# Edge pass: the last group's sum stands ahead of this group's build and shares its signal; the round of pairs signals once

## The chip, the cores and the metric

One Trainium2 chip, one of its cores. The metric is the device time of one execution in microseconds. The times before are 1935.26, 1936.90 and 1938.03 us, median 1936.9.

## The reference, cut to what matters

Four layers of a graph network work on 3125 nodes of 128 features and 103125 edges that are sorted by destination. The kernel's edge pass computes layer 0's edge part, and beside it the matrix of edge counts and weights between nodes that layers 1 to 3 use.

```
h = maximum(layernorm(x), 0)                                   # 3125 x 128
msg_input = concatenate([h[src], h[dst], edge_attr])           # 103125 x 288
t = relu(msg_input @ W1.T + b1)
messages = t @ W2.T + b2
agg = segment_sum(messages, dst, num_segments=3125)
upd = relu(agg @ Wu.T + bu)
x = x + layernorm_with_gamma_beta(h + upd)
...                                                            # layers 1 to 3: segment_sum(h[src], dst) and
                                                               # segment_sum(w * h[src], dst), matmuls, norms
```

## The kernel before

Before the edge pass the node products P = h @ W1 (source part) and Q = h @ W1 (destination part) are made and stored as pairs of f16 halves. The edge pass (`edge_pass`) then runs over 202 groups (`MG`) of 512 edges, four blocks of 128, and at the same time over 196 rounds (`J`) of pairs, one round for 16 destination nodes. Behind the groups come 9 more steps (`LAST`) for the last node tiles. Every engine has its own stream with a loop `for s in range(MG + LAST)`, and the order in each stream is written out by hand; engines meet at semaphores only.

In step s:

- POOL gathers the source rows of a group with four indirect DMAs (line 989), five groups ahead (`SLOTS_P`); `gather(g)` waits until `pre` tells that the build of group g - 5 is done.
- TensorE: `build(s)` makes the messages before the relu in one of two PSUM banks: 8 matmuls of 128x128 (line 1309) for the attributes and the destination side, then 2 of 128x512 (line 1314) that add the gathered rows through the identity. It waits for `cut` of group s - 2, which frees the bank, and signals `pre`. `multiply(s)` makes the round's matrix with 8 matmuls of 128x150 (line 1327) in three units of 3, 3 and 2; each unit goes to one of four PSUM banks in turn and signals `multiplied`. From the second unit on it waits for `weights_out` of the round before. `sum_up(s - 1)` adds the messages of the group before into a band of 64 destinations with 8 matmuls of 128x64 (line 1339), one PSUM bank for all groups. It waits for `cut` of its group, and for `added` of the group before its own, and signals `summed`.
- ACT: `matrix_out(s - 1)` reads the three units out of PSUM (lines 1236, 1241, 1244), then `relu(s)` (line 1228) makes the high half of the messages. Then it stores the round's weights by DMA.
- DVE: `hots(s + 1)` (lines 1007, 1009), `whole_weights(s - 1)` (line 1034, three), `pair_hots(s + 1)` (lines 1022, 1024, 1027, 1028), `low_parts(s)` (line 1043, signals `cut`), `add(s - 1)` (line 1054, signals `added`), in every fourth step `ea_low` (line 1062). For each of 25 node tiles `update`, `residual`, `normalise` and `low_of_tile` follow 2, 4, 6 and 8 steps after the tile's last group; `update` begins at line 1102 and `residual` at line 1116.
- SP loads the sides, bands, attributes and tile rows; its loads of sides and bands wait for `pre`.

After the edge pass come the later layers, which no line of the change touches.

Of the kernel before, what the change touches and what calls it, by code (L numbers as in the profile page):

```python
# [29 lines left out]
MG = -(-E // GE)  # L30
# [21 lines left out]
UNITS = -(-PAIRS // UNIT)  # L52
# [34 lines left out]
def blocks_of(g):  # L87

    return min(MB, USED - g * MB)
# [680 lines left out]
def edge_pass(nc, new, d):  # L770

    NS, NPRE, NPG, NAB = 3, 2, SLOTS_P, BANDS_HELD
    with ExitStack() as ctx:
# [44 lines left out]
        aw_stored = [new(f"aw_stored{k}") for k in range(3)]  # L818
        hot_t, hot_ds = new("hot_t"), new("hot_ds")
        equalled, hot_keys = new("equalled"), new("hot_keys")  # L820
        pre, relued, cut, summed, added = new("pre"), new("relued"), new("cut"), new("summed"), new("added")
        multiplied, halves_out, weights_out, counted = (new("multiplied"), new("halves_out"), new("weights_out"),
                                                        new("counted"))
        dve_step, flagged, checked, cleared = new("edge_dve"), new("flagged"), new("checked"), new("edge_cleared")
# [8 lines left out]
        def in_twos(grid):  # L833
            return grid.rearrange("p a (e o) -> p a e o", o=2)

        def every_row(row, n):
            return row.rearrange("p (a e o) -> p a e o", a=1, o=2).broadcast_to([P, n, row.shape[1] // 2, 2])

        def every_column(column, width):
            return column.rearrange("p a (e o) -> p a e o", e=1).broadcast_to([P, column.shape[1], width // 2, 2])  # L840
# [29 lines left out]
        for name, row in (("lo", iota_lo), ("band", iota_band), ("key", iota_key)):  # L870
            width = row.shape[1] // 2
            held_rows[name] = (psum[:, 7, at:at + width], row[:, :].bitcast(F32))
            at += width
        row_lo, row_band, row_key = (held_rows[name][0].bitcast(F16) for name in ("lo", "band", "key"))

        def whole_at(t):
            past = EDGE + (t + 1) * P
            return 1 + max(g for g in range(MG) if base_of(g) + EDGE < past)
# [14 lines left out]
        with nc.Block() as block:  # L893
# [103 lines left out]
            def _(dve):  # L997
                def hots(g):
                    q, s = g // QUAD, (g // QUAD) % NS
                    n = blocks_of(g)  # L1000
                    if g >= 3:
                        dve.wait_ge(summed, g - 2)
                    dve.wait_ge(rel_in[q % 2], 16 * (q // 2 + 1))
                    if q >= NS:
                        dve.wait_ge(pre, QUAD * (q - NS + 1))
                    at = slice((g % QUAD) * GE, (g % QUAD) * GE + n * P)
                    nc.vector.tensor_scalar(side[2 * ED:P, s, at], rel_row[2 * ED:P, q % 2, at], band_no[2 * ED:P, 0:1],
                                            None, ALU.is_equal).then_inc(hot_t, 1)
                    nc.vector.tensor_tensor(in_twos(hot_d[:, g % 3, 0:n]), every_row(row_band, n),
                                            every_column(rel_of[:, g * MB:g * MB + n], BAND), ALU.is_equal  # L1010
                                            ).then_inc(hot_ds, 1)

                def pair_hots(r):
                    u = r % 2
                    if r >= 2:
                        dve.wait_ge(multiplied, UNITS * (r - 1))

                    def field(k, width):
                        return every_column(fields[:, k, r * PAIRS:(r + 1) * PAIRS], width)

                    equal, times_w1, times_w2 = (in_twos(hot_key[:, u, :, q, :]) for q in range(3))
                    nc.vector.tensor_tensor(equal, every_row(row_key, PAIRS), field(A_KEY, PKEY),
                                            ALU.is_equal).then_inc(equalled, 1)
                    nc.vector.tensor_tensor(in_twos(hot_lo[:, u]), every_row(row_lo, PAIRS), field(A_LO, P),  # L1024
                                            ALU.is_equal)
                    dve.wait_ge(equalled, r + 1)
                    nc.vector.tensor_tensor(times_w1, equal, field(A_W1, PKEY), ALU.mult)
                    nc.vector.tensor_tensor(times_w2, equal, field(A_W2, PKEY), ALU.mult).then_inc(hot_keys, 1)
# [9 lines left out]
                def low_parts(g):  # L1038
                    n = blocks_of(g) * P
                    if g >= 2:  # L1040
                        dve.wait_ge(summed, g - 1)
                    dve.wait_ge(relued, g + 1)
                    nc.vector.scalar_tensor_tensor(out=msg_lo[:, g % 2, 0:n], in0=pre_of(g), scalar=0.0,  # L1043
                                                   in1=msg_hi[:, g % 2, 0:n], op0=ALU.max,
                                                   op1=ALU.subtract).then_inc(cut, 1)

                def add(g):
                    dve.wait_ge(summed, g + 1)
                    if g:
                        dve.wait_ge(added, g)  # L1050
                    else:
                        dve.wait_ge(cleared, 1)
                    at = slice(base_of(g) + EDGE, base_of(g) + EDGE + BAND)
                    nc.vector.scalar_tensor_tensor(out=agg[:, at], in0=agg_of(g), scalar=1 / S_MSG, in1=agg[:, at],  # L1054
                                                   op0=ALU.mult, op1=ALU.add).then_inc(added, 1)
# [151 lines left out]
            def _(act):  # L1207
# [15 lines left out]
                def relu(g):  # L1223
                    n = blocks_of(g) * P
                    act.wait_ge(pre, g + 1)
                    if g >= 2:
                        act.wait_ge(summed, g - 1)
                    nc.scalar.activation(msg_hi[:, g % 2, 0:n], pre_of(g), ACT.Relu).then_inc(relued, 1)  # L1228

                def matrix_out(r):  # L1230
                    if r >= 3:
                        act.wait_ge(aw_stored[r % 3], 16 * (r // 3))
                    for j in range(UNITS):
                        unit = UNITS * r + j
                        act.wait_ge(multiplied, unit + 1)
                        nc.scalar.activation(columns_of_unit(flat_adj[:, :, r * W:(r + 1) * W], j), third_of(r, j, 0),  # L1236
                                             ACT.Copy, saturate=True)
                        if unit:
                            act.wait_ge(counted, unit)
                        n = len(pairs_of(j))  # L1240
                        nc.scalar.activation(over_of[:, 0:n * PKEY].rearrange("p (t a) -> p t a", t=NT),  # L1241
                                             third_of(r, j, 0), ACT.Relu, bias=minus_most[:, 0:1],
                                             accum_out=over[:, unit:unit + 1]).then_inc(counted, 1)
                        nc.scalar.activation(columns_of_unit(  # L1244
                            aw_out[:, r % 3, :].rearrange("p (t n) -> p t n", t=NT), j), third_of(r, j, 1), ACT.Copy,
                            scale=1 / UP).then_inc(halves_out, 1)
# [49 lines left out]
            def _(pe):  # L1296
# [21 lines left out]
                def multiply(r):  # L1318
                    u = r % 2
                    pe.wait_ge(hot_keys, r + 1)  # L1320
                    for j in range(UNITS):
                        unit = UNITS * r + j
                        if unit >= RING:
                            pe.wait_ge(weights_out, unit - RING + 1)
                        for i, p in enumerate(pairs_of(j)):
                            thirds = bank_of(r, j).rearrange("p (q x) -> p q x", q=3)
                            done = nc.tensor.matmul(thirds[:, :, i * PKEY:(i + 1) * PKEY], hot_lo[:, u, p, :],  # L1327
                                                    hot_key[:, u, p], start=True, stop=True)
                        done.then_inc(multiplied, 1)

                def sum_up(g):
                    n = blocks_of(g)
                    pe.wait_ge(cut, g + 1)
                    pe.wait_ge(hot_ds, g + 1)
                    if g:
                        pe.wait_ge(added, g)
                    for part, msg in enumerate((msg_hi, msg_lo)):
                        for k in range(n):
                            done = nc.tensor.matmul(agg_of(g), msg[:, g % 2, k * P:(k + 1) * P], hot_d[:, g % 3, k, :],  # L1339
                                                    start=(part == 0 and k == 0), stop=(part == 1 and k == n - 1))  # L1340
                    done.then_inc(summed, 1)

                def await_rows(s):
                    pe.wait_ge(hot_ds, min(s + 2, MG))
# [19 lines left out]
                    nc.tensor.matmul(psum[:, 7, 0:D], agg[:, at], w2u[:, :], start=True, stop=True).then_inc(u_psum, 1)  # L1364

                for s in range(MG + LAST):
                    if s < MG:
                        build(s)
                    if s < J:
                        multiply(s)  # L1370
                    if 1 <= s <= MG:
                        sum_up(s - 1)
                    if s == 2:
                        await_rows(s)
                        fold_weights()
# [1664 lines left out]
```

## Time and profile before

| | us |
|---|---|
| timed runs, median of 3 | 1936.9 (1935.26 to 1938.03) |
| profiled execution, its span | 2170.3 |
| of it: edge pass, groups 0 to 200 | 130 to 1358 |
| of it: later layers | 1378 to 2170 |

The profiled execution is one other execution, with the profiler writing a record of each instruction and each semaphore update. Durations of single instructions are read from it, and its 2170.3 us stand beside the 1936.9 of the timed runs. The two are not the same amount, so every sum is made against the profiled execution first. In the rows, the time in square brackets is the idle time of the engine before an instruction with what ended it; "remote" is a semaphore update for which no instruction ends near it, "issue" a wait for nothing that the profile shows. Ends of matmuls are modelled.

### The profile page before, as it was taken

What the parts mean: (1) busy time and instruction counts of PE and PEld (TensorE: products, weight loads), DVE (VectorE), ACT (ScalarE), POOL (GpSimd) and SP (SyncE); (2) the same over time, 40 slices, a digit from 0 to 9 for tenths busy, and PEclk for the clock granted to TensorE, in tenths of its full rate; (3) what the DMA queues carried; (4) which work ended last, traced back from release to release, by engine and by line L of the source; (5) the groups of instructions that cost most, each with busy time, mean ns of one, the idle gap of its engine ahead of it and who ended that gap; (6) DMA issues with size and microseconds to landing.
All of it is one profiled execution on the core that took longest, in us unless ns stands there. A gap on an engine that the chain in (4) does not pass through costs nothing. (4 is left out here: it accounts for less than half of the span.)

```text
span 2170.3 us, 30067 instructions
## 1 busy us (share of the span) xinstructions
PE 1378.5 (64%) x9130; PEld 904.1 (42%) x9130; DVE 1129.6 (52%) x3500; ACT 812.2 (37%) x3272; POOL 841.7 (39%) x877
## 2 busy tenths in 40 slices
PE   3235444445445454545545445799899999899997
PEld 2123233333333333333333333356656666455444
DVE  7756666667667666666666666431442224311101
ACT  2235455555545555454545544111343432100000
POOL 5636666666666666666666665000000000000001
PEclk8566766666666666666665666899999999899999
DMA  6444434434443433434434443103100001871770
GB/s 198 143 96 116 115 113 116 122 115 121 121 116 112 122 120 114 118 113 122 119 112 117 120 119 103 30 12 139 34 29 1 10 7 39 305 266 65 264 293 29
DMA packets 200853, 245.67 MB, mean 113 GB/s; under 512 B 36794, under 2 KB 174053, under 8 KB 200674
## 3 DMA queue, kind: packets, MB, share of 16 engines
q1 hardware_dynamic: 142978, 137.56, 20.1%
q0 software_dynamic: 29472, 65.73, 11.7%
q10 hardware_dynamic: 28224, 40.15, 5.2%
q8 instruction: 93, 1.52, 0.3%
q14 instruction: 86, 0.70, 0.1%
HBM read 174.00 MB, written 55.93 MB: 106 GB/s over the span
## 5 line engine op out<-in xcount | busy, mean ns | idle before, releaser
L989 POOL DMA_INDIRECT arena<-dram_PHL,src_of x786 | 765.2, 974 | 472.1 <-remote 205.4
L1327 PE MATMUL psum<-arena 128*128 128x150 f16 x1568 | 238.9, 294 | 604.3 <-DVE aw_out L1034 330.4
L1327 PEld LDWEIGHTS psum<-arena 128*128 128x128 f16 x1568 | 153.4, 125 | 762.2 <-issue 380.6
L1228 ACT ACTIVATE arena<-psum 128x512 f16<-128x512 f32 x202 | 121.9, 603 | 429.3 <-remote 294.5
L1236 ACT ACTIVATE arena<-psum 128x150 fp8e4<-128x150 f32 (+1 forms) x588 | 173.6, 295 | 181.4 <-remote 93.8
L1241 ACT ACTIVATE arena<-psum,arena 128x150 f16<-128x150 f32 (+1 forms) x588 | 228.6, 389 | 1.6 <-remote 1.6
L1309 PE MATMUL psum<-arena 128*128 128x128 f16 x1612 | 182.2, 281 | 39.0 <-DMA arena<-dram_QHL 36.3
L1054 DVE SCALAR_TENSOR_TENSOR agg_all<-psum,agg_all 128x64 f32<-128x64 f32 x202 | 43.8, 217 | 283.4 <-remote 281.4
L1314 PE MATMUL psum<-arena 128*128 128x512 f16 x404 | 184.5, 552 | 3.6 <-issue 3.6
L1244 ACT ACTIVATE aw_out<-psum 128x150 f32<-128x150 f32 (+1 forms) x588 | 179.6, 305 | 0.0
L1043 DVE SCALAR_TENSOR_TENSOR arena<-psum,arena 128x512 f16<-128x512 f32 x202 | 137.9, 683 | 76.2 <-issue 41.3
L2489 PE MATMUL psum<-arena,parts_b 128*128 128x512 fp8e4 (+5 forms) x875 | 172.1, 356 | 4.4 <-PEq L2911 3.8
L2452 POOL DMA_DIRECT2D parts_a<-dram_x x7 | 5.3, 752 | 419.6 <-DMA dram_x<-parts_a 396.3
L1309 PEld LDWEIGHTS psum<-arena 128*128 128x128 f16 x1612 | 144.4, 131 | 40.5 <-issue 38.8
L1034 DVE SCALAR_TENSOR_TENSOR aw_out<-psum,aw_out 128x150 f32<-128x150 f32 (+1 forms) x588 | 140.6, 287 | 11.7 <-issue 10.5
L2602 PE MATMUL psum<-arena,parts_a 128*128 128x512 f32 (+2 forms) x350 | 134.4, 544 | 2.4 <-ACT late_aggT L2727 2.4
L2602 PE MATMUL psum<-arena,parts_b 128*128 128x512 f32 (+2 forms) x350 | 133.0, 539 | 1.1 <-ACT late_aggT L2727 1.1
L1024 DVE TENSOR_TENSOR arena<-psum,fields 128x1024 f16<-128x1024 f16 x196 | 133.1, 679 | 0.0
L1241 ACT ACTIVATION_READ_ACCUMULATOR arena<-psum,arena 128x1 f32 x588 | 132.9, 226 | 0.0
L2489 PEld LDWEIGHTS psum<-arena,parts_b 128*128 128x128 f16 (+1 forms) x875 | 89.8, 104 | 77.6 <-issue 6.6
L1339 PE MATMUL psum<-arena 128*128 128x64 f16 x1612 | 111.0, 226 | 7.1 <-DVE agg_all L1054 7.1
L1339 PEld LDWEIGHTS psum<-arena 128*128 128x128 f16 x1612 | 102.1, 123 | 10.5 <-issue 6.9
(344 smaller groups left out, 2080.3 us busy)
## 6 DMA issues: line engine op xcount, KB each, us to landing
dram_aw<-aw_out ACTq DMA_DIRECT2D x196, 200.0 KB
arena<-dram_aw SPq DMA_DIRECT2D x6, 6400.0 KB
arena<-dram_aw SPq DMA_DIRECT2D x3, 4800.0 KB
arena<-in_ea_quads SPq DMA_DIRECT2D x51, 256.0 KB
arena<-dram_rel SPq DMA_DIRECT2D x51, 256.0 KB
arena<-arena SPq DMA_DIRECT2D x408, 32.0 KB
arena<-dram_PHL,src_of POOLq DMA_INDIRECT x806
arena<-dram_aw SPq DMA_DIRECT2D x2, 4000.0 KB
```

Source lines behind the costliest of these rows:

```text
L989: nc.gpsimd.indirect_dma_start(gathered_p[:, slot, k, :], None, d["PHL"], bass.IndirectOffsetOnAxis(ap=src_of[:, b:b + 1], axis=0)).then_i ...
L1034: nc.vector.scalar_tensor_tensor(out=columns_of_unit(whole, j), in0=third_of(r, j, 2), scalar=1 / UP, in1=columns_of_unit(whole, j), op0=A ...
L1043: nc.vector.scalar_tensor_tensor(out=msg_lo[:, g % 2, 0:n], in0=pre_of(g), scalar=0.0, in1=msg_hi[:, g % 2, 0:n], op0=ALU.max, op1=ALU.sub ...
L1236: nc.scalar.activation(columns_of_unit(flat_adj[:, :, r * W:(r + 1) * W], j), third_of(r, j, 0), ACT.Copy, saturate=True)
L1241: nc.scalar.activation(over_of[:, 0:n * PKEY].rearrange("p (t a) -> p t a", t=NT), third_of(r, j, 0), ACT.Relu, bias=minus_most[:, 0:1], a ...
L1244: nc.scalar.activation(columns_of_unit(aw_out[:, r % 3, :].rearrange("p (t n) -> p t n", t=NT), j), third_of(r, j, 1), ACT.Copy, scale=1 / ...
L1309: nc.tensor.matmul(out[:, k * P:(k + 1) * P], side[:, s, at:at + P], node_side[:, g % NAB, part * D:(part + 1) * D], start=(part == 0 and ...
L1314: done = nc.tensor.matmul(out, ident_h[:, :], gathered_p[:, g % NPG, 0:n, part * D:(part + 1) * D], start=False, stop=(part == 1))
L1327: done = nc.tensor.matmul(thirds[:, :, i * PKEY:(i + 1) * PKEY], hot_lo[:, u, p, :], hot_key[:, u, p], start=True, stop=True)
L1339: done = nc.tensor.matmul(agg_of(g), msg[:, g % 2, k * P:(k + 1) * P], hot_d[:, g % 3, k, :], start=(part == 0 and k == 0), stop=(part == ...
L2489: last = nc.tensor.matmul(psum[0:width, SUM_BANK[n % 2], 0:end - first], parts.flat[:, t * parts.block + at:t * parts.block + at + width], ...
L2602: last = nc.tensor.matmul(psum[:, 0, 0:m * W], g[k][:, t, :], slab[:, slot_of(n), 0:m, t * W:(t + 1) * W], start=(t == 0), stop=(t == NT - 1))
```

## The change

Four things change. (1) TensorE's loop calls `sum_up(s - 1)` ahead of `build(s)` and `multiply(s)`; before it stood behind both. (2) `sum_up` no longer signals `summed`. Since matmuls finish in order, the signal `pre` of the build that follows it tells of it too: `pre` of group g + 1 is the (g + 2)nd. `hots`, `low_parts` and `add` wait for that; only the last group, which no build follows, has a signal of its own (`last_sum`). (3) `relu` waits for `pre` alone. (4) `multiply` signals `multiplied` once for a round instead of once for a unit; `matrix_out` and `pair_hots` wait for the round.

```diff
@@ -872,6 +872,9 @@
+        def pre_with_sum(g):
+            return g + 2
@@ -999,7 +1002,7 @@
                     if g >= 3:
-                        dve.wait_ge(summed, g - 2)
+                        dve.wait_ge(pre, pre_with_sum(g - 3))
@@ -1013,7 +1016,7 @@
                     if r >= 2:
-                        dve.wait_ge(multiplied, UNITS * (r - 1))
+                        dve.wait_ge(multiplied, r - 1)
@@ -1038,14 +1041,17 @@
                     if g >= 2:
-                        dve.wait_ge(summed, g - 1)
+                        dve.wait_ge(pre, pre_with_sum(g - 2))
                     dve.wait_ge(relued, g + 1)
...
                 def add(g):
-                    dve.wait_ge(summed, g + 1)
+                    if g + 1 < MG:
+                        dve.wait_ge(pre, pre_with_sum(g))
+                    else:
+                        dve.wait_ge(last_sum, 1)
@@ -1223,16 +1229,14 @@
                     act.wait_ge(pre, g + 1)
-                    if g >= 2:
-                        act.wait_ge(summed, g - 1)
...
                 def matrix_out(r):
                     if r >= 3:
                         act.wait_ge(aw_stored[r % 3], 16 * (r // 3))
+                    act.wait_ge(multiplied, r + 1)
                     for j in range(UNITS):
                         unit = UNITS * r + j
-                        act.wait_ge(multiplied, unit + 1)
@@ -1326,7 +1330,7 @@
-                        done.then_inc(multiplied, 1)
+                    done.then_inc(multiplied, 1)
@@ -1338,7 +1342,8 @@
-                    done.then_inc(summed, 1)
+                    if g == MG - 1:
+                        done.then_inc(last_sum, 1)
@@ -1364,12 +1369,12 @@
                 for s in range(MG + LAST):
+                    if 1 <= s <= MG:
+                        sum_up(s - 1)
                     if s < MG:
                         build(s)
                     if s < J:
                         multiply(s)
-                    if 1 <= s <= MG:
-                        sum_up(s - 1)
```

## Rows read from the trace of the kernel before

**Rows 1.** Busy time by stage: stretch, length, each engine, granted clock, DMA
```profile
core 0: us, PE busy (x) PEld busy (x) DVE busy (x) ACT busy (x) POOL busy (x), PEclk, DMA share, GB/s
...
130.00:1358.00 1228.00, 590.86 (x5230) 426.36 (x5228) 813.53 (x2571) 618.88 (x2796) 765.24 (x786) 0.66 0.41 117
...
1378.00:2170.00 792.00, 748.28 (x3660) 447.81 (x3658) 211.54 (x659) 160.26 (x414) 12.84 (x16) 0.97 0.29 104
```

**Rows 2.** Waits of the edge pass: who waited for whom, total us, times, longest
```profile
ACT arena L1228 <- remote: 294.5, 118, 4.8
DVE agg_all L1054 <- remote: 281.4, 70, 7.3
...
POOL arena L989 <- remote: 205.4, 117, 3.1
```

**Rows 3.** Timeline of one step: start, us, engine, line, what [idle before, releaser]
```profile
659.69 0.39 PE L1339 MATMUL psum<-arena 128*128 128x64 f16 x8
...
663.15 0.30 ACT L1236 ACTIVATE arena<-psum 128x150 fp8e4<-128x150 f32 x1 [1.26 <-remote]
...
665.24 0.30 ACT L1236 ACTIVATE arena<-psum 128x150 fp8e4<-128x150 f32 x1 [1.25 <-PE psum L1327]
...
667.37 0.25 ACT L1236 ACTIVATE arena<-psum 128x100 fp8e4<-128x100 f32 x1 [1.28 <-issue]
...
668.87 0.23 DVE L1054 SCALAR_TENSOR_TENSOR agg_all<-psum,agg_all 128x64 f32<-128x64 f32 x1 [7.05 <-remote]
```

**Rows 4.** The gathers as a group: count, busy us, mean ns, idle before
```profile
L989 POOL DMA_INDIRECT arena<-dram_PHL,src_of x786 | 765.2, 974 | 472.1 <-remote 205.4 <-issue 196.1 <-PE psum L1314 70.6
```

**Rows 5.** Timeline of POOL: the first two gathers and the last
```profile
130.62 0.94 POOL L989 DMA_INDIRECT arena<-dram_PHL,src_of  x1 [21.92 <-PE psum L1314]
131.87 1.04 POOL L989 DMA_INDIRECT arena<-dram_PHL,src_of  x1 [0.30 <-issue]
...
1345.05 0.94 POOL L989 DMA_INDIRECT arena<-dram_PHL,src_of  x1 [0.31 <-issue]
```

**Rows 6.** Timeline of TensorE at the lower clock: sum, build's end, first unit
```profile
671.27 0.64 PE L1339 MATMUL psum<-arena 128*128 128x64 f16 x8
...
672.55 1.06 PE L1314 MATMUL psum<-arena 128*128 128x512 f16 x2
...
673.41 0.58 PE L1327 MATMUL psum<-arena 128*128 128x150 f16 x3
```

**Rows 7.** Timeline of ACT: a relu, then a round's first and last instruction
```profile
656.82 0.60 ACT L1228 ACTIVATE arena<-psum 128x512 f16<-128x512 f32 x1 [2.82 <-remote]
...
657.31 0.29 ACT L1236 ACTIVATE arena<-psum 128x150 fp8e4<-128x150 f32 x1
...
658.02 0.32 ACT L1236 ACTIVATE arena<-psum 128x150 fp8e4<-128x150 f32 x1
...
659.19 0.32 ACT L1244 ACTIVATE aw_out<-psum 128x100 f32<-128x100 f32 x1
```

**Rows 8.** Timeline of DVE over one step in which it hardly waits
```profile
657.52 0.69 DVE L1043 SCALAR_TENSOR_TENSOR arena<-psum,arena 128x512 f16<-128x512 f32 x1
658.13 0.21 DVE L1054 SCALAR_TENSOR_TENSOR agg_all<-psum,agg_all 128x64 f32<-128x64 f32 x1
...
659.72 0.35 DVE L1022 TENSOR_TENSOR arena<-psum,fields 128x400 f16<-128x400 f16 x1
...
661.14 0.68 DVE L1043 SCALAR_TENSOR_TENSOR arena<-psum,arena 128x512 f16<-128x512 f32 x1
```

**Rows 9.** Timeline of DVE: an update and a residual, each to the next group's work
```profile
673.10 0.33 DVE L1102 SCALAR_TENSOR_TENSOR tail_y<-b2u_rows,arena,bu_rows 128x128 f32<-128x128 f32 x1
...
674.78 0.35 DVE L1007 TENSOR_SCALAR arena<-arena 64x512 f16<-64x512 f16 x1
...
1345.71 0.15 DVE L1116 RECIPROCAL arena<-arena 128x1 f32<-128x1 f32 x1
...
1347.91 0.35 DVE L1007 TENSOR_SCALAR arena<-arena 64x512 f16<-64x512 f16 x1
```

More of the change, by code:

```diff
@@ L820, in edge_pass @@
         equalled, hot_keys = new("equalled"), new("hot_keys")
-        pre, relued, cut, summed, added = new("pre"), new("relued"), new("cut"), new("summed"), new("added")
+        pre, relued, cut, last_sum, added = new("pre"), new("relued"), new("cut"), new("last_sum"), new("added")
         multiplied, halves_out, weights_out, counted = (new("multiplied"), new("halves_out"), new("weights_out"),
```

## The prediction

> **What bounds the kernel now.** I read the stages first, then the waits of the edge pass, then the steps row by row. The stages [rows 1]: the edge pass is 1228 of 2170.3 us, 202 steps of 6.1 us, and no engine is full in it: DVE is busy for 814 us, POOL for 765, ACT for 619, TensorE for 591. The late layers take 792 us with TensorE busy for 748, and nothing of the change is in them. So the question is what a step waits for.
>
> The waits [rows 2] point at TensorE's signals: DVE stands 281.4 us before `add`, ACT 294.5 before `relu`, POOL 205.4 before a gather, each "remote", that is, a semaphore update with no instruction ending near it. In the rows of one step [rows 3] the eight matmuls of `sum_up` end at 660.08, and DVE, which waits for nothing but `summed`, begins `add` at 668.87. The multiplies of that round stand before the sum, so they too were done by 660; yet ACT, whose three units follow each other every 0.7 us where it is not held [rows 7], starts them at 663.15, 665.24 and 667.37. The matmuls were done and their signals came about 2 us apart. Five signals of TensorE leave a step (`pre`, three times `multiplied`, `summed`), and this is what the change goes at.
>
> **Does that queue of signals stand in the timed runs?** The profiled execution took 2170.3 us and the median of the timed runs is 1936.9: 233.4 us less. Where can they be missing? In the late layers TensorE is idle for only 792 - 748 = 44 us [rows 1]; those matmuls don't shrink. The 130 us ahead of the pass can give some 14 if they shrink as the whole did. So at least 175 of the 233 are missing from the edge pass, which then takes at most 1053 us, 5.2 per step. What would be left if no signal were late? The gathers: 786 of them [rows 4], the first starts at 130.62, the next 1.25 later, the last at 1345.05 [rows 5]. Back to back they take 1.25 us each when quiet, or the mean duration of 0.974 plus the 0.30 between two, 1.274: 982.5 to 1001 us, 5.0 to 5.1 per step. The last then ends at 1113 to 1132 instead of 1346.0, so 233 to 214 us earlier, and the execution takes 2170.3 - 233 = 1937 to 1956. The timed 1936.9 is the lower of these to half a microsecond. I take it that in the timed runs POOL issues gathers without a pause and the late signals are a product of the profiling. The Trainium skill fits that ("NOTIFIC — the notification-queue block", section "Overflow: three behaviours, one of which stalls the engine": the block's internal pipeline holds producers back rather than lose a record); no row here shows that block.
>
> **The change, part by part**, against 5.0 us per step of gathers.
>
> *One signal for a round's pairs.* TensorE gives 588 - 196 = 392 fewer increments, which costs it nothing. ACT starts `matrix_out` after the eighth matmul instead of the third: at the slow clock three take 0.58 us [rows 6], so five take 0.97. ACT's work for a round is 2.2 us (657.31 to 659.51) and its `relu` 0.6 [rows 7], 2.8 of a step of 5.0, so 0.97 is covered. DVE's `pair_hots` already needed all three units.
>
> *The sum ahead of the build, without a signal.* `sum_up` and `build` are the same instructions; only their order changes, no DMA moves with them, and 201 increments go. `hots`, `low_parts` and `add` wait for `pre` instead. `relu` has made DVE pass that value by the time of `low_parts`, so `add` waits for nothing more. The wait that is new in effect is TensorE's: `build(s)` stands behind `sum_up(s-1)`, which waits for `low_parts(s-1)` and for `add(s-2)`. Behind it are queued `multiply(s)`, and for `pre` wait `relu`, POOL's gather five groups on and SP's loads. The loops that this closes, with TensorE at the slow clock:
> - One step: `low_parts` to `add` 0.61 (657.52 to 658.13), `add` 0.21 [rows 8]; sum and build 671.27 to 673.61, 2.34 [rows 6]; `relu` 0.60, and 0.10 from its end to `low_parts` [rows 7, 8], taken for each of three hand-overs. 0.61 + 0.21 + 2.34 + 0.60 + 0.30 = 4.06.
> - Two steps, from a build's end: eight multiplies 1.55 (8/3 of 0.58), `matrix_out` 2.2, the last `whole_weights` about 0.2, `pair_hots` 1.42 (659.72 to 661.14), `low_parts` 0.61, `add` 0.21, sum and build 2.34, five hand-overs 0.5: 9.0, or 4.5 per step.
> - DVE alone: 3.62 from one `low_parts` to the next [rows 8]. An `update` adds 1.68 and a `residual` 2.20 [rows 9], each in 25 of 202 steps. Where these stand, the step is 0.82 + 2.8 + 1.7 or 2.2, about 5.3 and 5.8; with six others of 4.5, eight steps take 38.1, 4.76 per step.
>
> Before the change the first two loops aren't closed and DVE alone gives 3.62 + 0.124 x 3.88 = 4.1. So the change spends some 0.65 us per step, at the slow clock, of a slack of 0.9, and the gathers (1010 us for 202 steps, against 962) still come last. A gather waits for the build five groups back, so POOL doesn't feel one step of 5.8. Part sums: signals 0; later `matrix_out` 0; order 0. At the pass's end `sum_up(200)` leaves the place behind `build(201)`, at most 0.6 us, and it is hidden beside `relu`. Bounds: below, nothing but a late signal can be gained, 0 to 44 us (rival 1); above, 0 to 100 us (rival 2).
>
> **Rivals.** *1, faster:* some of the late signals are there without the profiler too. The pass could hold up to 44 us above the gathers if the late layers lost all their idle time in the timed runs. For: the rows show real waits. Against: the sum of the gathers leaves nothing. With half of it gone: 1936.9 - 22 = 1915. By the Trainium skill ("TensorE: Matmul & The Clock Gate", section "The cost: per-tile semaphore tail") increments of TensorE serialise at some 26 ns each; an estimate from that is 593 x 0.026 = 15 us if they were on the path, against 0 by my rows, where gathers cover them.
>
> *2, slower:* the new order becomes the bound: TensorE, held behind `sum_up(s-1)`, starts the build too late and POOL runs out of free slots. It decides from a mean step above 5.0, thus if a step costs 0.25 more than my 4.76. For: DVE's tile steps already stand above 5.0, and the clock was granted at 0.66, mostly the slow level [rows 1]. Against: all prices above are the slow clock's. At 5.15 per step it is 202 x 0.15 = 30 us: 1967. With only the 50 tile steps showing by 0.3 us: 1952.
>
> *3, it does nothing where it counts,* which is my forecast: the profiled execution gets shorter, since three of five signals are gone from each step, and the timed runs don't.
>
> **The numbers.** Forecast 1937 with 0.62 (within 0.2%, 1933 to 1941, about what a measurement of this kernel can tell from no change); rival 1 0.18; rival 2 0.20. The range goes to 1915 and 1960: it takes in half of rival 1, and of rival 2 what is below 0.11 us per step.
>
> **What would show it.** In the profile after: "remote" before `add` (281.4) near zero, as its wait is over before it; fewer of them before `relu` and POOL; the profiled span clearly shorter than 2170, between 1940 and 2100; POOL's 0.30 gaps in more of its rows. The forecast is wrong if the timed runs follow the profiled span downward (rival 1), or if the rows show TensorE idle before `sum_up` for `low_parts` or `add` while POOL waits for `pre` (rival 2).

## The result and the profile after

The changed kernel takes 1941.05 us (median of 20 runs, 1935.62 to 1944.54), the kernel before 1937.62 (20 runs, 1933.02 to 1941.11). The ratio is 1.0016, 95% interval [1.0009, 1.0023]: within the 0.2% that was forecast, and on the slow side of no change.

One fact has to stand ahead of every row, because the prediction missed it: the time of this kernel goes with the chip that it runs on. The kernel before took 1937.6, 1935.8, 1936.6 and 1939.4 us in four sets of runs, and 2157.4 (27 runs, 2152.8 to 2161.1) and 2172.7 (7 runs) on two other chips, where each of its runs was as long. By its length the profiled execution of before, 2170.3 us, belongs to the second kind of chip; which chip it ran on isn't on record. Its timed runs of 1936.9 and the profile after belong to the first. I call them the quick and the late kind. No chip was used at two separate times, so "chip" could also stand for something else that was the same through one set of runs.

The stages of the changed kernel's profile (stretch, length, busy time of TensorE, weight loads, DVE, ACT, POOL, granted clock, DMA):

```profile
core 0: us, PE busy (x) PEld busy (x) DVE busy (x) ACT busy (x) POOL busy (x), PEclk, DMA share, GB/s
130.00:1128.00 998.00, 611.73 (x5233) 430.54 (x5233) 819.48 (x2570) 619.62 (x2796) 753.05 (x786) 0.64 0.50 144
1149.00:1941.00 792.00, 747.88 (x3658) 447.64 (x3656) 211.58 (x659) 160.35 (x414) 12.84 (x16) 0.97 0.30 104
```

Beside [rows 1] the edge pass is 998 us instead of 1228, and the late layers are 792 as before (TensorE busy for 748 us in both). The gathers as a group (count, busy, mean ns, idle before), and the waits of the pass (who waited for whom, total us, times, longest), of the changed kernel:

```profile
L992 POOL DMA_INDIRECT arena<-dram_PHL,src_of x786 | 753.0, 958 | 265.9 <-issue 237.8
```

```profile
ACT arena L1232 <- PE psum L1318: 321.1, 173, 40.1
...
POOL arena L992 <- issue: 237.8, 780, 0.3
PE psum L1343 <- DVE agg_all L1060: 205.9, 185, 2.5
...
POOL arena L992 <- PE psum L1318: 28.2, 6, 24.0
```

Three things are to be seen. POOL's idle time is 780 gaps of 0.3 us, the issue itself: it gathers without a pause, where [rows 2] had it wait 205.4 us for signals. `relu` waits for the build and no longer for anything "remote". And the wait that the change creates is there: TensorE stands 205.9 us, in 185 of 201 steps, before `sum_up` for DVE's `add`, which follows `low_parts` directly. It costs POOL a pause in one place only (experiment 5).

The trace of the kernel before on a chip of the quick kind (experiment 5) is the right partner of this one. Its edge pass, in the window of the same length, and its waits, then `relu` over the whole pass (count, duration in ns, first and last start in us) in this trace and in the one that the prediction was read from:

```profile
130.00:1128.00 998.00, 571.98 (x5247) 428.78 (x5244) 821.54 (x2592) 608.21 (x2798) 750.81 (x786) 0.70 0.50 144
```

```profile
PE psum L1314 <- DMA arena<-dram_PHL,src_of: 309.1, 145, 4.6
...
POOL arena L989 <- issue: 237.2, 778, 0.3
...
DVE agg_all L1054 <- PE psum L1339: 0.6, 1, 0.6
```

```profile
L1228 ACT ACTIVATE arena<-psum x202: 383/597/761, 130.5 to 1123.7; 128x512 f16<-128x512 f32 x101
...
L1228 ACT ACTIVATE arena<-psum x202: 383/597/672, 130.4 to 1358.1; 128x512 f16<-128x512 f32 x101
```

The same kernel's pass is 993 us long on the one kind and 1228 on the other. From the last `relu` to the end it is 807 and 812 us, and the instructions themselves are as fast: the median `relu` is 597 ns in both, the median gather 944 ns.

So the kernel before, too, was already a row of gathers without a pause, TensorE waiting 309.1 us for their rows. On this kind of chip there was no late signal for the change to remove. In the changed kernel part of that idle time has only moved, from the wait for gathered rows to the wait for `add`.

### The profile page after: what moved, and what is told of

Same layout as the page of the kernel before. It is cut to its first block and busy times, and to the rows that moved or that the text cites. A ratio compares the mean times of both kernels' runs of the same rounds, so it can differ in the third digit from the quotient of the medians.

```text
span 1940.9 us, 29867 instructions
## 1 busy us (share of the span) xinstructions
PE 1399.7 (72%) x9130; PEld 908.6 (47%) x9130; DVE 1135.5 (59%) x3500; ACT 813.2 (42%) x3272; POOL 830.5 (43%) x877
## 5 line engine op out<-in xcount | busy, mean ns | idle before, releaser
L992 POOL DMA_INDIRECT arena<-dram_PHL,src_of x786 | 753.0, 958 | 265.9 <-issue 237.8
L1343 PE MATMUL psum<-arena 128*128 128x64 f16 x1612 | 104.4, 221 | 216.5 <-DVE agg_all L1060 206.7
L1331 PE MATMUL psum<-arena 128*128 128x150 f16 x1568 | 218.2, 307 | 43.2 <-DVE aw_out L1037 43.2
L1037 DVE SCALAR_TENSOR_TENSOR aw_out<-psum,aw_out 128x150 f32<-128x150 f32 (+1 forms) x588 | 150.5, 290 | 34.2 <-ACT aw_out L1248 28.2
L2732 ACT COPY late_aggT<-psum 128x512 f32<-128x512 f32 (+2 forms) x14 | 7.5, 533 | 255.0 <-PE psum L2607 255.0
```

The source lines that it names most:

```text
L992: nc.gpsimd.indirect_dma_start(gathered_p[:, slot, k, :], None, d["PHL"], bass.IndirectOffsetOnAxis(ap=src_of[:, b:b + 1], axis=0)).then_i ...
L1037: nc.vector.scalar_tensor_tensor(out=columns_of_unit(whole, j), in0=third_of(r, j, 2), scalar=1 / UP, in1=columns_of_unit(whole, j), op0=A ...
```

## The experiments

All ratios are to the kernel before on the same chip. Experiments 1 to 3 ran on the chip of 2157.4 us.

**1. The order alone**, all five signals kept. Late kind of chip.

```diff
+                    if 1 <= s <= MG:
+                        sum_up(s - 1)
                     if s < MG:
                         build(s)
                     if s < J:
                         multiply(s)
-                    if 1 <= s <= MG:
-                        sum_up(s - 1)
```

> The kernel before with one edit: TensorE calls sum_up(s-1) ahead of build(s); all five signals of a step stay. Theory A (the gathers bound the timed runs; the 3.4 us that the change adds are one pause of POOL before the gathers of group 9, 2.6 us in the profile after, because build(4) now stands behind the sum that waits for low_parts(3)): ratio 1.0015, about 1940.5 us timed, and a pause of 2 to 3 us of the same kind. Theory B (the added time comes with the changed signals): ratio 1.000. Of the profiled execution: if the late signals go by their number, its span stays above 2100 us, as five signals leave each step; if they go by the order, it falls to about 1941.

Measured: 2160.7 us against 2157.4, ratio 1.0015 [1.0006, 1.0024]. The number is that of theory A, but the ground had moved under it: this chip is late in every run, and on it POOL pauses in most groups, so the ratio can't be put down to the one pause of theory A. The span of 2156 us, against 2157.4 for the kernel before here, says that the order alone doesn't take the lateness away; of the profiler it says nothing. The order alone, with its gathers, was not run on a quick chip.

**2. The pairs' signal alone**, three signals a step. Same chip.

```diff
-                        dve.wait_ge(multiplied, UNITS * (r - 1))
+                        dve.wait_ge(multiplied, r - 1)
...
+                    act.wait_ge(multiplied, r + 1)
                     for j in range(UNITS):
                         unit = UNITS * r + j
-                        act.wait_ge(multiplied, unit + 1)
...
-                        done.then_inc(multiplied, 1)
+                    done.then_inc(multiplied, 1)
```

> The kernel before with one edit: multiply signals multiplied once for a round; the order and the signal of the sum stay, so three signals a step in place of five. Theory A: timed ratio 1.000 (0.999 to 1.001), as 0.97 us later in matrix_out is covered. Theory B: 1.001 to 1.002. Of the profiled execution: if the late signals go by their number, the span lies between 1937 and 2100 us, nearer to 1937; if they go by the order, it stays near 2170.

Measured: 2156.8 us, ratio 0.9997 [0.9987, 1.0007]. The later start of `matrix_out` is covered, and two signals fewer change nothing in the time. Waits of 200 to 1300 us, of the kernel before (the trace of 2170.3 us) and then of this one:

```profile
ACT arena L1228 <- remote: 270.7, 107, 4.8
...
DVE agg_all L1054 <- remote: 246.5, 62, 7.0
POOL arena L989 <- remote: 184.6, 106, 3.1
```

```profile
DVE agg_all L1054 <- remote: 251.8, 55, 6.7
ACT arena L1228 <- remote: 224.7, 101, 5.4
...
POOL arena L989 <- remote: 173.5, 103, 2.6
```

`add` waits as long as before, `relu` 46 us and POOL 11 us less. A queue of signals that went by their number would have given back far more: two of five are gone, and the time is the same.

**3. One load earlier**, in the changed kernel and in the kernel before. Late kind of chip.

```diff
+                        if q == 0:
+                            load_edges(2)
                         if q + 1 < QUADS:
                             load_sides(q + 1)
                             load_bands(q + 1)
                         if q + 2 < QUADS:
-                            load_edges(q + 2)
+                            if q:
+                                load_edges(q + 2)
```

> The changed kernel with SP's load of the attributes of quad 2 moved ahead of the loads of sides and bands of quad 1, in step 0 alone. In the profile after, ACT waits 4.5 us for these attributes and DVE 4.3 us for ACT, just ahead of the pause of POOL. Theory A: the pause of 2.6 us before group 9 goes, and the ratio to the kernel before is 1.000 (0.999 to 1.0005). If the cost is spread over the steps or stands at the end of the pass instead: it stays at 1.0016.

> The kernel before with the same move of the one load. Theory A: build(4) doesn't wait for low_parts(3) in the old order, so there is little or no pause to gain: ratio 1.000 (0.9993 to 1.0003). If the early load helps whatever the order: as much as it gives the changed kernel, some 0.9985.

Measured: the changed kernel with it 2166.5 us, 1.0045 [1.0031, 1.0058]; the kernel before with it 2158.3, 1.0002 [0.9993, 1.0011]. The first is a miss. On a chip where POOL pauses in most groups the one pause can't be seen, so the test was void there and was made again for the changed kernel (experiment 7); the kernel before with the early load has no run on a quick chip. It shows one thing more: with only two signals a step the changed kernel, with this load moved, is no quicker on the late kind of chip, at 2166.5 us it is slower than the kernel before. Why it was 0.3% slower than the order alone there is open.

**4. Three gathers a group instead of four**, in both kernels. The rows of every fourth block are left out and old ones used. A third chip, also of the late kind (the kernel before 2172.7 us).

```diff
+        def gathers_of(g):
+            return blocks_of(g) if g < NPG else min(blocks_of(g), 3)
...
-                    for k in range(blocks_of(g)):
+                    for k in range(gathers_of(g)):
...
-16 * sum(blocks_of(k) for k in range(g % NPG, g + 1, NPG))
+16 * sum(gathers_of(k) for k in range(g % NPG, g + 1, NPG))
```

> The kernel before, with three gathers in place of four for each group from the fifth on: the rows of every fourth block are left out (old rows of the slot are used in their place). POOL's floor falls from 5.0 to 3.8 us per step, so the other loops show. If the gathers bound the timed runs: the time falls until DVE's own 4.1 to 4.4 us per step is the bound, by 202 x 0.6 to 0.9 = 120 to 180 us, to 1757 to 1817. If they don't: it stays near 1937.

> The changed kernel with the same gathers left out. By the loops of the prediction (4.76 us per step with the sum ahead of the build, at the slow clock) the time falls by only 202 x 0.25 = 50 us, to about 1890, so 70 to 130 us slower than the kernel before with the same cut. If the loop with the sum ahead costs less than worked out there (the clock at its higher level, or hand-overs shorter): within 40 us of the kernel before with the same cut.

Measured: 1935.4 us, 0.891 [0.889, 0.893], and 1932.9 us, 0.889 [0.887, 0.891]. Both expected times are missed; what came true is the other branch of the second text, that the two kernels are within 40 us of each other. That the time with three gathers is the quick kind's time with four is chance: it is made of other steps. The stretch 200 to 1000 us, with four gathers (experiment 2's kernel, on the chip of 2157.4 us) and with three (the kernel before, on this chip):

```profile
200.00:1000.00 800.00, 375.88 (x3438) 271.07 (x3438) 541.83 (x1713) 406.53 (x1853) 508.54 (x524) 0.69 0.42 119
```

```profile
200.00:1000.00 800.00, 448.82 (x4191) 322.28 (x4190) 653.32 (x2089) 498.25 (x2273) 463.01 (x479) 0.71 0.46 132
```

524 gathers are 131 groups, 6.1 us each; 479 are 160 groups, 5.0 us each. The difference of 1.1 us is about one gather (1.25). On this kind of chip a step is the gathers' issue plus about 1.2 us: 4 x 1.25 + 1.1, 3 x 1.25 + 1.25 (the trace of 2170.3 us has 517 gathers in this stretch, 6.2 us a step). The rows of the kernel before show what the rest is. A step of its trace, on POOL, TensorE, ACT:

```profile
308.47 0.63 PE L1339 MATMUL psum<-arena 128*128 128x64 f16 x8
...
309.06 0.94 POOL L989 DMA_INDIRECT arena<-dram_PHL,src_of  x1 [0.31 <-issue]
...
309.68 0.59 PE L1314 MATMUL psum<-arena 128*128 128x512 f16 x2
...
311.35 0.60 ACT L1228 ACTIVATE arena<-psum 128x512 f16<-128x512 f32 x1 [3.89 <-PE psum L1314]
...
311.59 0.95 POOL L989 DMA_INDIRECT arena<-dram_PHL,src_of  x1 [1.59 <-PE psum L1314]
311.84 0.29 ACT L1236 ACTIVATE arena<-psum 128x150 fp8e4<-128x150 f32 x1
```

The build ends at 310.27, its signal reaches ACT at 311.35, 1.35 us after POOL's last gather ended, and the next gather follows at 311.59. In [rows 3] the queue is let go in the same way: POOL's last gather ended at 667.04, and at 668.87 to 669.04 came the sum, the build and a multiply together. I read this as theory C: beside gathers in flight TensorE's signals come late, they come through once POOL has to pause, and POOL pauses because it waits for one of them. It fits these rows and isn't shown, since no late chip ran without gathers.

**5. Both kernels again, unedited**, on a chip of the quick kind.

> The changed kernel, nothing edited, beside the kernel before on whatever chip this is. So far the kernel before took 1937 us on one chip and 2157 and 2173 on two others, all its runs alike, and there the order alone gave 1.0015, the pairs' signal alone 0.9997. Theory C (on some chips TensorE's signals don't get through while a gather is in flight, and POOL, once it waits for a build, lets them through; both kernels then run at four gathers and one flush per step): on such a chip the changed kernel takes 2155 to 2163 us, ratio 0.999 to 1.003, and its steps are 6.1 us; on the other kind 1941, ratio 1.0016. Against it (fewer signals help where signals are late): well under 2150 on a chip where the kernel before takes 2157 or more.

> The kernel before, nothing edited, for its own trace on this chip. On a chip of the 1937 kind: POOL's gaps of 0.30 in nearly all rows, relu within 0.1 us of the build's end, a pause of POOL before the gathers of group 9 shorter than the 2.6 us of the changed kernel by 2 to 3 us if that pause is the added time. On a chip of the other kind: the trace that the prediction was read from, 6.1 us per step, signals 2 us late.

Measured: the changed kernel 1940.8 us, 1.0026 [1.0017, 1.0035]; the kernel before as a kernel of its own 1937.7, 1.0009 [0.9998, 1.0021], which is how far the same kernel can stand from itself. POOL's waits for the build in the changed kernel (this is its second trace) and in the kernel before:

```profile
POOL arena L992 <- PE psum L1318: 28.5, 7, 23.2
```

```profile
POOL arena L989 <- PE psum L1314: 26.2, 8, 24.1
```

The longest is the start of the pass in both. What is left is 5.3 us in 6 waits and 2.1 us in 7, and 0.3 of each wait is the issue. In the changed kernel one row holds nearly all of it. Changed kernel, 144 to 155 us:

```profile
144.14 0.63 ACT L1219 ACTIVATE arena<-arena 128x512 f16<-128x512 f32 x1 [4.76 <-DMA arena<-in_ea_quads]
...
150.94 0.69 DVE L1046 SCALAR_TENSOR_TENSOR arena<-psum,arena 128x512 f16<-128x512 f32 x1
...
151.90 0.58 PE L1343 MATMUL psum<-arena 128*128 128x64 f16 x8 [1.82 <-DVE agg_all L1060]
...
152.30 1.04 PE L1313 MATMUL psum<-arena 128*128 128x128 f16 x8
...
153.13 1.06 PE L1318 MATMUL psum<-arena 128*128 128x512 f16 x2
...
154.46 0.94 POOL L992 DMA_INDIRECT arena<-dram_PHL,src_of  x1 [3.73 <-PE psum L1318]
```

Kernel before, the same groups:

```profile
142.24 0.63 ACT L1213 ACTIVATE arena<-arena 128x512 f16<-128x512 f32 x1 [5.97 <-DMA arena<-in_ea_quads]
...
149.03 0.69 DVE L1043 SCALAR_TENSOR_TENSOR arena<-psum,arena 128x512 f16<-128x512 f32 x1
...
149.24 1.06 PE L1314 MATMUL psum<-arena 128*128 128x512 f16 x2
...
149.95 0.94 POOL L989 DMA_INDIRECT arena<-dram_PHL,src_of  x1 [0.30 <-issue]
...
151.20 0.94 POOL L989 DMA_INDIRECT arena<-dram_PHL,src_of  x1 [0.30 <-issue]
```

In the kernel before the build of group 4 runs beside `low_parts(3)` and ends at 150.30, as POOL is in the last gather of group 8 (149.95 to 150.89); group 9 follows at 151.20 without a pause. In the changed kernel `sum_up(3)` has to come first, it waits for `low_parts(3)` and `add(2)`, and the build ends at 154.19. POOL, with its five slots used up, stands for 3.73 us before group 9, 3.43 more than its usual gap. It is the only such row of the pass; in the first trace it was 2.90, thus 2.6 more.

The new order is only half of why the build is 3.9 us later. From ACT's start on the attributes (144.14 and 142.24) to the end of build(4) it takes 10.05 us in the changed kernel and 8.06 before: these 2.0 us are the order's, nearly all of them the 1.82 us that `sum_up(3)` waits. The other 1.9 us are there already when the attributes arrive. SP sends for them behind four loads of bands, and these four took 3.35 to 3.80 us in all five traces with the new order on quick chips, and 2.5 us in the two with the old. Why they take longer is open.

The gathers themselves sum to 753.0 and 754.9 us in the changed kernel's two traces and to 750.8 here. With a single trace of the kernel before this can't be told from scatter.

**6. No gathers at all from the fifth group on**, rows of the first groups used again; the same two kernels, and then the order alone.

```diff
-            return blocks_of(g) if g < NPG else min(blocks_of(g), 3)
+            return blocks_of(g) if g < NPG else 0
```

> The kernel before without any gather from the fifth group on (the rows of the first five groups stay in the slots and are used again; the output is not the reference's). Theory C: with no gather in flight no signal is late on any chip: relu starts within 0.1 us of the build's end, and the step is what DVE's own chain gives, 4.1 to 4.4 us: 2 x 65 us of the ends plus 202 x 4.2, in all 1760 to 1830 us on either kind of chip. If the late signals come from something else (the profiler's records, the number of TensorE's signals): they stay, and the step stays above 4.9 on a chip of the slow kind.

> The changed kernel with the same gathers left out. Theory C and the loops of the prediction: no signal late, and the step is 4.76 us against 4.2 of the kernel before with the same cut, 80 to 110 us more, 1870 to 1920 us. If the loop that the new order closes costs less than worked out: within 50 us of the kernel before with the same cut.

> The kernel before with the sum ahead of the build and all five signals kept, and without any gather from the fifth group on (output not the reference's). On a chip where the kernel before takes 1937 us: the order alone closes the loop, so 1850 to 1865 us, as the changed kernel with the same cut (1858.8), and not 1823; if the pairs' single signal made part of the added 36 us, it lies between. On a chip where it takes 2157 or more, theory C (signals are late only beside gathers in flight): no late signal, steps of 4.6 us, and again about 1860 us; if they are late without gathers too, steps stay near 6 us or above 4.9, and the time above 1920.

Measured: before 1823.1 us, 0.942 [0.940, 0.944]; changed 1858.8, 0.960 [0.958, 0.962]; order alone (on another quick chip) 1854.4, 0.957 [0.955, 0.959]. The first and the third lie in their expected ranges; the second is below its 1870 to 1920, so the loop costs less than worked out. All three ran on the quick kind, so what theory C says of the late kind without gathers stays untried. But the covered loops are measured. `relu` as a group, 200 to 1000 us, of before and changed:

```profile
L1231 ACT ACTIVATE arena<-psum 128x512 f16<-128x512 f32 x183 | 115.4, 631 | 71.8 <-PE psum L1317 71.7
```

```profile
L1235 ACT ACTIVATE arena<-psum 128x512 f16<-128x512 f32 x173 | 105.8, 612 | 156.2 <-PE psum L1321 156.2
```

183 and 173 steps in 800 us are 4.37 and 4.62 us. Over the whole pass the first and last `relu` are 878.6 and 921.7 us apart, 4.37 and 4.59 us a step. So the change costs 0.21 to 0.25 us a step once the gathers don't cover it, 36 us in the timed runs, and the order alone costs 31; the intervals of the last two overlap, so nothing is shown for the signals. In the same stretch TensorE waits, before, for `whole_weights`, and changed, for `add`:

```profile
PE psum L1330 <- DVE aw_out L1037: 304.1, 163, 8.9
```

```profile
PE psum L1346 <- DVE agg_all L1063: 237.7, 166, 2.5
```

**7. One load earlier in the changed kernel, again**, now on the quick kind; the diff is that of experiment 3.

> The changed kernel with the one load of attributes moved ahead in SP's step 0, once more, for a chip where the kernel before takes 1937 us. There the changed kernel had one pause of POOL, 2.6 and 3.4 us in two traces, before the gathers of group 9, and the kernel before had none. If the late attributes in ACT's and DVE's step 2 are its cause: no pause, and a ratio to the kernel before of 1.000 to 1.001 in place of 1.0016 and 1.0026. If the pause comes from the new order's own start: it stays at 2.5 us or more. On a chip of the other kind (2157 us or more) the comparison doesn't tell this; there the rows tell again whether signals are late.

Measured: 1936.9 us against 1936.6, ratio 1.0002 [0.9993, 1.0011]. The changed kernel's loss is gone: this interval lies below that of experiment 5, [1.0017, 1.0035]. Its rows around groups 3 and 4:

```profile
138.02 0.63 ACT L1222 ACTIVATE arena<-arena 128x512 f16<-128x512 f32 x1
...
147.02 1.06 PE L1321 MATMUL psum<-arena 128*128 128x512 f16 x2
...
148.11 0.60 ACT L1235 ACTIVATE arena<-psum 128x512 f16<-128x512 f32 x1 [2.13 <-PE psum L1321]
...
148.25 0.94 POOL L995 DMA_INDIRECT arena<-dram_PHL,src_of  x1 [0.30 <-issue]
...
149.49 1.06 POOL L995 DMA_INDIRECT arena<-dram_PHL,src_of  x1 [0.30 <-issue]
```

ACT has the attributes at 138.02, without a wait, where the changed kernel without this edit waited for them until 144.14. The build of group 4 is done at 148.1 instead of 154.2, and behind the first gather no gap of POOL is longer than its issue, though TensorE still waits for `add` before the sum. So the pause needs the late attributes. The edit takes away all of their delay, not only the 1.9 us by which they were later than in the kernel before, so it doesn't weigh the two halves of experiment 5 against each other.

## Why the prediction was right, and where it was not

**The bound: right.** The sum said that the timed 1936.9 us are gathers back to back at 1.25 us. The trace of the kernel before on the quick kind has 778 gaps of 0.3 us and no other wait of weight, and from its first gather to its last it is 989 us (130.8 to 1119.9), against the 982.5 to 1001 worked out. Both kernels hang on the same row of gathers, so neither fewer signals nor the order could gain.

**"The late signals are a product of the profiling": wrong.** This step had the right remainder, 233 us that the timed runs lack, and the wrong owner. The profiled execution of the changed kernel took 1942.75 us, inside its 20 runs, so profiling costs nothing that can be seen, and on the late kind of chip every run is as long as the profiled one. What differed between 2170.3 and 1936.9 was, by all that the later runs show, the chip. The argument by elimination (not the late layers, not the front, hence the edge pass) was sound and is confirmed, 1228 against 993 us for the same kernel; the list of causes behind it was too short. So the forecast hit although one of its two supports was wrong: what carried it was the sum of the gathers. The rule that I put beside it, from the Trainium skill's "NOTIFIC — the notification-queue block", section "Overflow: three behaviours, one of which stalls the engine", has no sign in any run here: no execution was longer for being profiled.

**Rival 3's mark, "the profiled execution gets shorter": wrong in its reason.** The span did fall to 1940.9, within the 1940 to 2100 that I gave, but it was taken on the quick kind of chip. The same goes for the end of the "remote" waits. With two (one load moved), three or five signals a step the late kind gives 2166, 2157 and 2157 to 2161 us.

**The pairs' signal: right.** Nothing, 0.9997 [0.9987, 1.0007], measured on a late chip only.

**The new loop: right mechanism, wrong size.** Predicted 4.1 us per step before and 4.76 after, so 0.65 more; without the gathers it is 4.37 and 4.62, 0.25 more. I see two terms that were off; no run prices them one by one. DVE's own chain was taken too short: its waits for ACT, which waits for attributes, are in 4.37 and not in 3.62 + 0.48 (41.5 us in the 183 steps without gathers, 0.23 a step). And the sum and the build were priced at the slow clock throughout, while the granted clock without gathers was 0.82 before and 0.73 after. That both are below 5.0 was right and was what the forecast needed.

**"POOL doesn't feel one step of 5.8": wrong.** This is where the 3.4 us come from. The slots give POOL a lead of five groups, but near the start of the pass ACT and DVE wait 4.8 and 4.6 us for attributes that land late, and this uses the lead up. In the old order the build of group 4 was then done 0.6 us before POOL's last gather of group 8 had ended. The new order put the sum, and its wait for `low_parts(3)` and `add(2)`, in front of that build, and the attributes came 1.9 us later besides. That is rival 2's mechanism in one place, made up in half by a later load that the sum of the prediction had at nothing ("no DMA moves with them"). I had the rival decide "from a mean step above 5.0"; it decides earlier, wherever the lead is used up, and its price was one pause of 2.6 to 3.4 us and not 15 or 30. Of the ratio 1.0016, 3.1 us, that chip's own trace shows 2.6 as the pause; in the second comparison (1.0026, 5.0 us) it is 3.4, and the 1.6 us more stay within what a kernel differs from itself.

## What to carry to other kernels

Work out the bound from the cadence of the one queue that never rests, here 786 gathers at 1.25 us, and hold the timed runs against it before pricing any wait: waits under such a row cost nothing, whatever their sum. When a profiled execution and the timed runs differ by far more than the runs among themselves (here 12% against 0.5%), first ask whether they ran on the same chip, by running the unedited kernel once more beside the next experiment. A change that takes away an engine's lead over another should be walked through the first few steps and not only through the mean one: the lead that the mean step promises can be used up near the start, and there a single late load decides.

## What the runs showed of the hardware

- Chips differ by 11 to 12% on this kernel (2157.4 and 2172.7 us against 1936 to 1939), all but a few us of it in the stage with indirect gathers (1228 against 993 us from the first `relu` to the last) and none to speak of in the layers behind it (812 and 807 us). Single instructions are as fast on both kinds. Within one chip the runs of one kernel agree within 0.5%.
- On the late kind, in the steps read here, matmuls' semaphore updates come about 2 us apart ([rows 3]) or in bunches 1.3 to 2 us after POOL's last gather (311.35 after 310.00, 668.87 to 669.04 after 667.04). The step is the gathers' issue plus 1.1 to 1.25 us, at four gathers and at three. With two, three and five signals of TensorE a step there are 521, 524 and 517 to 524 gathers in 800 us. That gathers in flight hold the signals back fits every row read here and is not shown: no run on such a chip went without gathers.
- On the quick kind `relu` starts as the build ends (kernel before in experiment 5: build until 150.30, `relu` at 150.33).
